# Releasing the projection matmuls before the state decay, and keeping the mixer output in halves

## The chip, the cores and the metric

The kernel runs on the 8 NeuronCores of one Trainium2 chip. All cores run the same program on different data and don't talk to each other. The metric is device time in microseconds of the slowest core, from one execution of the whole program. In all texts PE is TensorE, DVE is VectorE, ACT is ScalarE, POOL is GpSimd and SP is SyncE.

## The reference, cut to what matters

For x of shape (4, 4096, 1024), with 4 heads of width 256:

```
xn = layernorm(x)
q, k, v = silu(xn Wq^T), silu(xn Wk^T), silu(xn Wv^T)      # per head 256 wide
f = log_sigmoid(xn Wf^T) / 8 ;  s = 1 - exp(f)
S1[t] = S1[t-1] * exp(f[t]) + k[t] (x) s[t] ;  ok = q . S1
qv = softmax(ok)
S2[t] = S2[t-1] * exp(f[t]) + s[t] (x) v[t] ;  ov = qv . S2
attn = rmsnorm(silu(ov)) * g_w @ Wo^T
out = x + attn + ffn(xn)      # ffn with quantized weights and activations, inner width 4096
```

## The kernel before

A core takes one batch entry (two cores share one) and runs three stages. Stage 1 (to about 1023 us) quantizes the three FFN weight matrices. Stage 2, the mixer, goes over all 4096 tokens twice: pass `hpg` 0 handles heads 0 and 1, pass 1 handles heads 2 and 3. A pass is a loop over 32 chunks of 128 tokens. Stage 3 (from about 3733 us) is the FFN, the output projection and the sum for the core's own 2048 tokens.

Each engine executes its own instructions in the order in which the program emits them, and engines wait for each other by counting semaphores. Nothing reorders the work: what stands first in the code of an engine holds up all that follows on it. In iteration `c` of a pass the code is emitted in this order:

- `emit_LN(c+1)`: POOL issues the load of the x block (L394), DVE takes the statistics (L403 to L411), ACT takes a square root (L418), DVE writes the normalized block (L430), SP issues its transposing DMA (L441). An x block has two buffers, so the load for chunk c+1 can be issued once chunk c-1 has been normalized.
- `chainA(c-1, 0)`, which starts the part of the previous chunk that doesn't depend on earlier chunks.
- `emit_A2a(c)`: on PE the projections F and K of this chunk, 16 matmuls of 512 columns into `ps_f` and `ps_k` (L467). They wait for the transposed x block and for the mark `M[c-1]["state"]`. Then ACT computes softplus from F (L476, L478), PE forms its cumulative sum and its column sum (L486 into `ps_g`, L488 into `ps_m2`), ACT takes four exponentials (L496 to L502), PE projects Q and V (L511 into `ps_q`, 32 matmuls of 128 columns, and L516 into `ps_v`, 8 of 512), PE turns the total decay into a column and spreads it over the partitions (L528, L532, again into `ps_g`), ACT takes the SiLU of Q, K and V (L540 to L542), DVE forms the gated `stb` (L553 to L557), PE transposes K (L568).
- `chainB` to `chainE` of chunk c-1 for both heads: score, softmax over the 256 slots (ACT L717), second read-out, SiLU into `ov_sb` (ACT L804). Between them `emit_B1_mm(c)` computes the state update of this chunk into `ps_q`, `ps_k`, `ps_v` and `ps_f`, the same four PSUM banks that the projections use.
- `emit_B1_vec(c)` on DVE: for each of the two heads 4 additions of the update in PSUM to the running state (L611, L616, into the buffer `tmpu`) and then 8 multiplications by the decay, which write the f32 state and its bf16 copy (L625 to L638). The multiplications of `s1` read the decay from `ps_g`. The end of all is `M[c]["state"]`.

So the projections of chunk c+1 have to wait for DVE, since the additions read the banks that they overwrite. A helper `S.guard` makes an engine wait for its own last instruction; each head has one between its additions and its multiplications, and one stands between the heads.

`ov_sb` holds the output of a whole pass, 4 blocks of 128 x 4096 in bf16 (4 MB). It is cleared at the start of a pass (L375), together with the states, and written to DRAM by one DMA at its end (L883). The four projection weights of pass 2 are loaded behind that DMA on the same queue, and so is the first x block; the first x block of stage 3 is issued once the last such DMA has landed.

Of the kernel before, what the change touches and what calls it, by code (L numbers as in the profile page):

```python
# [7 lines left out]
F32 = mybir.dt.float32  # L8
F32R = mybir.dt.float32r
BF16 = mybir.dt.bfloat16  # L10
# [5 lines left out]
T = 4096  # L16
# [32 lines left out]
def build_nc(nch=NCH, do_ffn=True, do_ag=True, dbg=(), mix_stop=0):  # L49
# [20 lines left out]
    d_ccout = nc.dram_tensor("cc_out", [1024, T], BF16)  # L70
# [9 lines left out]
    with es:  # L80
# [18 lines left out]
        block = es.enter_context(nc.Block())  # L99
# [227 lines left out]
        s2f = sbB("s2f", [128, 1024], F32)  # L327
        s1b = sbB("s1b", [128, 3 * 1024], BF16)
        s2b = sbB("s2b", [128, 3 * 1024], BF16)
        tmpu = sbB("tmpu", [128, 1024], F32)  # L330
        sf = tmpu[:, 512:1024]
        ov_sb = sbB("ov_sb", [128, 4 * T], BF16)

        ps_q = pstB("ps_q", [128, 512])
        ps_k = pstB("ps_k", [128, 512])
# [13 lines left out]
        dump_marks = []  # L349
        mk_state = 0  # L350
        for hpg in range(1 if mix_stop else 2):
# [28 lines left out]
            M = {}  # L380
# [68 lines left out]
            def emit_A2a(c):  # L449
# [4 lines left out]

                @block.tensor
                def _(t, pp=pp, c=c, gi=gi,
                      mk_prev=M.get(c - 1, {}).get("state", mk_state0h)):
                    S.wait(t, f"qt{pp}", mk_xnT_hist[gi])
                    S.wait(t, "dv", mk_prev)
                    if c == 0:  # L460
                        S.wait(t, "qw", mk_wload_h)
                        S.wait(t, "gp", mk_masks)
                        if dump_marks:
                            S.wait(t, "qst", dump_marks[-1])
                    for dst_ps, wsb in ((ps_f, wf_b), (ps_k, wk_b)):
                        for dc in range(8):
                            i = t.matmul(out=dst_ps[:], lhsT=xnTs(dc),  # L467
                                         rhs=wsb[:, dc * 512:(dc + 1) * 512],
                                         start=(dc == 0), stop=(dc == 7))
                        S.inc(i, "pe")  # L470
# [9 lines left out]
                mk_spf = S.val("sc")  # L480

                @block.tensor
                def _(t, mk_spf=mk_spf, mk_pst=M.get(c - 1, {}).get("st", 0)):
                    S.wait(t, "sc", mk_spf)
                    S.wait(t, "dv", mk_pst)
                    t.matmul(out=ps_g[:], lhsT=utones[:], rhs=spf[:],  # L486
                             start=True, stop=True)
                    i = t.matmul(out=ps_m2[0:1, 0:512], lhsT=ones_col[:], rhs=spf[:],  # L488
                                 start=True, stop=True)
                    S.inc(i, "pe")  # L490
# [110 lines left out]
            def emit_B1_vec(c):  # L601
                wsl = (c % 3) * 1024
                mk_u = M[c]["u"]

                @block.vector
                def _(v, mk_u=mk_u, wsl=wsl):
                    for h, (pu1, pu2) in enumerate(((ps_q, ps_k), (ps_v, ps_f))):
                        S.wait(v, "pe", mk_u - 1 + h)
                        for dkh in range(2):
                            sl = slice(h * 512 + dkh * 256, h * 512 + (dkh + 1) * 256)  # L610
                            v.tensor_tensor(out=tmpu[:, dkh * 256:(dkh + 1) * 256],  # L611
                                            in0=pu1[:, dkh * 256:(dkh + 1) * 256],
                                            in1=s1f[:, sl], op=ALU.add)
                        for mh in range(2):
                            sl = slice(h * 512 + mh * 256, h * 512 + (mh + 1) * 256)
                            i = v.tensor_tensor(out=tmpu[:, 512 + mh * 256:768 + mh * 256],  # L616
                                                in0=pu2[:, mh * 256:(mh + 1) * 256],
                                                in1=s2f[:, sl], op=ALU.add)
                        S.guard(v, i, "dv")
                        for dkh in range(2):  # L620
                            sl = slice(h * 512 + dkh * 256, h * 512 + (dkh + 1) * 256)
                            slw = slice(wsl + h * 512 + dkh * 256,
                                        wsl + h * 512 + (dkh + 1) * 256)
                            ts = tmpu[:, dkh * 256:(dkh + 1) * 256]
                            v.tensor_tensor(out=s1f[:, sl], in0=ts,  # L625
                                            in1=ps_g[:, h * 256:(h + 1) * 256],
                                            op=ALU.mult)
                            v.tensor_tensor(out=s1b[:, slw], in0=ts,  # L628
                                            in1=ps_g[:, h * 256:(h + 1) * 256],
                                            op=ALU.mult)  # L630
                        for mh in range(2):
                            sl = slice(h * 512 + mh * 256, h * 512 + (mh + 1) * 256)
                            slw = slice(wsl + h * 512 + mh * 256,
                                        wsl + h * 512 + (mh + 1) * 256)
                            ts = tmpu[:, 512 + mh * 256:768 + mh * 256]
                            v.tensor_scalar_mul(out=s2f[:, sl], in0=ts,
                                                scalar1=dccol[:, h * 2 + mh:h * 2 + mh + 1])
                            i = v.tensor_scalar_mul(out=s2b[:, slw], in0=ts,  # L638
                                                    scalar1=dccol[:, h * 2 + mh:h * 2 + mh + 1])
                        if h == 0:  # L640
                            S.guard(v, i, "dv")
                        else:
                            S.inc(i, "dv")
                M[c]["state"] = S.val("dv")

            def chainA(c, h, mk_extra=0):
# [125 lines left out]
            def chainE(c, h):  # L772
                sl2 = (c % 2) * 512
                hs = sl2 + h * 256
                rsl = ((c - 1) % 3) * 1024

                @block.tensor
                def _(t, h=h, hs=hs, mk_btm=M[c][f"btm{h}"], rsl=rsl):
                    S.wait(t, "dv", mk_btm)
                    for vh in range(2):  # L780
                        t.matmul(out=ps_i[:, 256 + vh * 128:256 + (vh + 1) * 128],
                                 lhsT=Vb[:, hs + vh * 128:hs + (vh + 1) * 128],
                                 rhs=btm[:], start=True, stop=False)
                        for mh in range(2):
                            i = t.matmul(out=ps_i[:, 256 + vh * 128:256 + (vh + 1) * 128],
                                         lhsT=s2b[:, rsl + h * 512 + mh * 256 + vh * 128:
                                                  rsl + h * 512 + mh * 256 + (vh + 1) * 128],
                                         rhs=qtT[:, mh * 128:(mh + 1) * 128],
                                         start=False, stop=(mh == 1))
                    S.inc(i, "pe")  # L790
                mk_ovp = S.val("pe")

                @block.vector
                def _(v, mk_ovp=mk_ovp):
                    S.wait(v, "pe", mk_ovp)
                    i = v.tensor_copy(out=eok[:], in_=ps_i[:, 256:512])  # L796
                    S.inc(i, "dv")
                mk_ove = S.val("dv")

                @block.scalar  # L800
                def _(sc, h=h, c=c, mk_ove=mk_ove):
                    S.wait(sc, "dv", mk_ove)
                    for vh in range(2):
                        i = sc.activation(  # L804
                            out=ov_sb[:, (2 * h + vh) * T + c * 128:
                                      (2 * h + vh) * T + (c + 1) * 128],
                            in_=eok[:, vh * 128:(vh + 1) * 128],
                            func=AF.Silu)
                    S.inc(i, "sc")

            emit_LN(0)
            for c in range(nch):
# [38 lines left out]
                if c >= 1:  # L851
# [4 lines left out]
                    chainD(c - 1, 1, stc)  # L856
                    chainE(c - 1, 1)
                emit_B1_vec(c)
            if mix_stop:
                mk_state = mk_state0h  # L860
            else:
# [16 lines left out]
            @block.gpsimd  # L878
            def _(g, hpg=hpg):
                S.wait(g, "dv", S.val("dv"))  # L880
                S.wait(g, "sc", S.val("sc"))
                S.wait(g, "qst", S.val("qst"))
                g.dma_start(out=d_ccout.ap()[hpg * 512:(hpg + 1) * 512, :]  # L883
                            .rearrange("(g p) t -> p g t", p=128),
                            in_=ov_sb[:].rearrange("p (g t) -> p g t", g=4)
                            ).then_inc(S.h["qst"], 16)
            S.c["qst"] += 16
            dump_marks.append(S.val("qst"))


# [637 lines left out]
```

## Time and profile before

| | us |
|---|---|
| median of 2 runs | 6448.29 (6443.7 to 6452.88) |
| the profiled execution | 6462.67 |
| its span on the slowest core, core 4 | 6461.1 |
| spans of the 8 cores | 6414.4 to 6461.1 |

Rows of a timeline give the start in us from the span's start and the duration in us; several equal instructions in sequence are merged (x8), and the bracket says how long the engine had been idle before and what it waited for. Rows of a group give busy us and mean ns of one, and after the bar the idle time just before them. The ends of matmuls are modelled and can overlap by some tenths of a us. The granted clock is given as a share of 2.4 GHz, so 0.50 is 1.2 GHz.

### The profile page before, as it was taken

Reading aid. Unit: us, or ns where it says so; the run is one execution under the profiler, and the core shown is the slowest. Engines: PE = TensorE matmul, PEld = TensorE weight load, DVE = VectorE, ACT = ScalarE, POOL = GpSimd, SP = SyncE. Lnnn points to the kernel's source line nnn. Section 1 sums busy time; section 2 is a strip of 40 time slices with the busy share of each in tenths; the row PEclk is TensorE's granted clock in tenths of the full one; section 3 lists DMA queues with packets and bytes.
Section 4 is the critical chain, followed back from the end, with each engine's and each line's share of the span. In section 5 each row is a group of like instructions: output and inputs, shape, how many; then the busy total and the mean of one; then the engine's idle time right before and its main releaser. Section 6 shows DMA issues by size and latency. Waiting matters only on the chain.

```text
span 6461.1 us, 37843 instructions; the slowest of 8 cores (6414.4 to 6461.1 us)
## 1 busy us (share of the span) xinstructions
PE 2429.7 (38%) x10934; PEld 1081.2 (17%) x10934; DVE 2156.4 (33%) x4980; ACT 1436.4 (22%) x2000; POOL 335.4 (5%) x583
## 2 busy tenths in 40 slices
PE   0000002444444424444444425552545254624553
PEld 0000001222222212222222212110211121111111
DVE  2222213444444444444444432213231323132222
ACT  0000001444444424444444412001210021001200
POOL 0000110000000000000000000110001000100010
PEclk9999999666666656666666667656765587557755
DMA  4443223000000021000000021222113211312131
GB/s 149 162 155 128 92 88 78 20 20 20 20 20 20 17 57 28 20 20 20 20 20 20 9 88 52 59 78 65 52 52 91 59 54 48 96 53 62 49 86 51
DMA packets 201145, 371.57 MB, mean 58 GB/s; under 512 B 127216, under 2 KB 135408, under 8 KB 193776
## 3 DMA queue, kind: packets, MB, share of 16 engines
q0 software_dynamic: 80880, 331.39, 16.1%
q1 hardware_dynamic: 120064, 37.76, 2.8%
q8 instruction: 94, 1.54, 0.1%
q14 instruction: 107, 0.88, 0.0%
HBM read 314.58 MB, written 41.94 MB: 55 GB/s over the span
## 4 chain that ended last, share of the span: by engine, by line
PE 26%; DMA 26%; DVE 25%; ACT 13%; issue 9%; DVEq 1%; POOLq 0%; ACTq 0%; SPq 0%; POOL 0%
DMA wdslab<-wdq_s 6%; PE pd L1109 5%; PE pd L1299 4%; DMA wtmp<-wdT 4%; PE pd L1115 3%; PE ps_f L467 3%; DMA wslab<-wuq_s 3%; DMA wslab<-wgq_s 3%; ACT L717 3%; DMA wtmp<-wuT 2%; DMA wtmp<-wgT 2%; DVE mpart L207 2%; DVE tmpu L611 1%; ACT L1127 1%; DVE s1b L628 1%
## 5 line engine op out<-in xcount | busy, mean ns | idle before, releaser
L1109 PE MATMUL pd<-xqTg,wslab 128*128 128x512 bf16 x1024 | 362.8, 518 | 768.3 <-DVE guT L1145 290.2
L1299 PE MATMUL pd<-wdslab,gcvt 128*128 128x512 bf16 x1024 | 452.0, 596 | 357.9 <-DMA wdslab<-wdq_s 236.6
L467 PE MATMUL ps_f<-wf_b,xnT 128*128 128x512 bf16 x512 | 227.0, 624 | 916.0 <-DVE s2b L638 514.6
L418 ACT ACT_TABLE_LOAD x64 | 82.1, 1283 | 1633.5 <-DVE lncol L411 1633.5
L1145 DVE TENSOR_TENSOR guT<-pd,sgT 128x512 f32<-128x512 f32 x128 | 88.5, 692 | 847.9 <-ACT sgT L1127 847.9
L1127 ACT ACT_TABLE_LOAD x128 | 164.2, 1283 | 898.2 <-PE pd L1115 898.2
L804 ACT ACT_TABLE_LOAD x128 | 164.2, 1283 | 622.2 <-DVE eok L796 622.2
L1416 ACT ACT_TABLE_LOAD x16 | 20.5, 1283 | 1255.9 <-DVE rrow L1407 1255.9
L1115 PE MATMUL pd<-xqTg,wslab 128*128 128x512 bf16 x1024 | 284.0, 427 | 0.0
L1109 PEld LDWEIGHTS pd<-xqTg,wslab 128*128 128x128 bf16 x1024 | 114.6, 120 | 990.3 <-issue 952.6
L223 PE MATMUL ps_w<-ones_col,mcol 128*1 128x1 f32 x6 | 0.6, 163 | 733.9 <-DVE mcol L216 733.9
L1287 DVE CAST gcvt<-guqT 128x256 bf16<-128x256 int8 x256 | 74.5, 293 | 589.7 <-PE pd L1299 589.3
L739 PE MATMUL ps_m<-identb,qtb 128*128 128x128 bf16 x256 | 47.6, 288 | 532.4 <-DVE qtb L727 532.4
L467 PEld LDWEIGHTS ps_f<-wf_b,xnT 128*128 128x128 bf16 x512 | 66.5, 139 | 1036.8 <-issue 1036.8
L1299 PEld LDWEIGHTS pd<-wdslab,gcvt 128*128 128x128 bf16 x1024 | 110.8, 125 | 697.6 <-issue 691.8
L280 DVE TENSOR_SCALAR wi<-wtmp,swcol 128x1024 int8<-128x1024 f32 (+1 forms) x48 | 61.7, 1286 | 457.0 <-DMA wtmp<-wdT 233.7
L717 ACT ACT_TABLE_LOAD x128 | 164.2, 1283 | 221.0 <-DVE smcol L699 221.0
L207 DVE TENSOR_REDUCE mpart<-wtmp 128x1 f32<-128x1024 f32 (+1 forms) x48 | 109.8, 2286 | 290.5 <-DMA wtmp<-wdT 140.3
L1276 POOL DMA_DIRECT2D wdslab<-wdq_s x256 | 138.0, 539 | 865.6 <-PE pd L1299 865.6
L553 DVE COPY dccol<-ps_m 128x4 f32<-128x4 f32 x64 | 10.4, 162 | 486.9 <-PE ps_g L532 486.9
L467 PE MATMUL ps_k<-wk_b,xnT 128*128 128x512 bf16 x512 | 156.4, 460 | 0.0
L394 POOL DMA_DIRECT2D xin<-x x64 | 34.0, 532 | 2251.2 <-DVE stT L670 2213.8
(194 smaller groups left out, 5017.3 us busy)
## 6 DMA issues: line engine op xcount, KB each, us to landing
wdslab<-wdq_s POOLq DMA_DIRECT2D x256, 256.0 KB, 2.9
wtmp<-wgT POOLq DMA_DIRECT2D x16, 2048.0 KB, 8.9
wtmp<-wuT POOLq DMA_DIRECT2D x16, 2048.0 KB, 8.8
wtmp<-wdT POOLq DMA_DIRECT2D x64, 512.0 KB, 3.5
xin<-x POOLq DMA_DIRECT2D x64, 512.0 KB, 5.0
wslab<-wgq_s POOLq DMA_DIRECT2D x32, 1024.0 KB, 6.1
wslab<-wuq_s POOLq DMA_DIRECT2D x32, 1024.0 KB, 6.1
wgq_s<-wqb POOLq DMA_DIRECT2D x8, 1024.0 KB, 4.1
```

The costliest lines, as they stand in the source:

```text
L207: i = v.reduce_sum(out=mpart[:, it:it + 1], in_=wtmp[:, :tw], axis=AXX, apply_absolute_value=True)
L418: i = sc.activation(out=lncol[:, 3:4], in_=lncol[:, 6:7], func=AF.Sqrt)
L467: i = t.matmul(out=dst_ps[:], lhsT=xnTs(dc), rhs=wsb[:, dc * 512:(dc + 1) * 512], start=(dc == 0), stop=(dc == 7))
L717: i = sc.activation(out=eok[:], in_=okf[:], func=AF.Exp, bias=smcol[:, 0:1], accum_out=smcol[:, 1:2])
L804: i = sc.activation(out=ov_sb[:, (2 * h + vh) * T + c * 128: (2 * h + vh) * T + (c + 1) * 128], in_=eok[:, vh * 128:(vh + 1) * 128], func= ...
L1109: i = t.matmul(out=pd[0][:, 0:512], lhsT=wslab[:, gbase + dc * 512 + isl * 128: gbase + dc * 512 + (isl + 1) * 128], rhs=xqTg[:, dc * GTOK ...
L1115: i = t.matmul(out=pd[0][:, 512:1024], lhsT=wslab[:, ubase + dc * 512 + isl * 128: ubase + dc * 512 + (isl + 1) * 128], rhs=xqTg[:, dc * G ...
L1127: i = sc.activation(out=sgT[:], in_=pd[0][:, 0:512], func=AF.Silu, scale=inv_swg[:])
L1145: i = v.tensor_tensor(out=guT[:, sl_id * GTOK:(sl_id + 1) * GTOK], in0=pd[0][:, 512:1024], in1=sgT[:], op=ALU.mult)
L1276: g.dma_start(out=wdslab[:, ppd * 1024:(ppd + 1) * 1024], in_=d_wdq[dc * 128:(dc + 1) * 128, :]).then_inc(S.h[f"qd{ppd}"], 16)
L1287: i = v.tensor_copy(out=gcvt[:, ppd * 256:(ppd + 1) * 256], in_=guqT[:, dc * GTOK + sg * 256: dc * GTOK + (sg + 1) * 256])
L1299: i = t.matmul(out=pd[sg * 2 + bi2][:, half * 512:(half + 1) * 512], lhsT=gcvt[:, ppd * 256 + bi2 * 128: ppd * 256 + (bi2 + 1) * 128], rhs ...
```

## The change

In `emit_B1_vec` the DVE work is split. All 8 additions of both heads come first, into a buffer `tmpa` of twice the size (each head has its own half), and their end is a new mark `M[c]["uev"]`. DVE then waits once for its own additions and does all 16 multiplications; their end remains `M[c]["state"]`. The number and the shapes of the DVE operations are the same; of the three own waits one is left.

The F and K projections of the next chunk now wait for `uev` instead of `state`. The cumulative-sum matmul, which overwrites `ps_g`, now waits for `state` (before, for the earlier mark `st`, since the projections ahead of it had waited for `state`).

`ov_sb` now holds half a pass (2 MB). In iteration 16, after `emit_B1_vec(16)`, POOL waits for ACT's last SiLU and writes the first half to DRAM; ACT waits for that DMA before it writes the output of chunk 16. The second half is written at the end of the pass. In POOL's program the new DMA stands ahead of the load of the x block of chunk 18.

```diff
@@ -327,9 +327,9 @@
         s2f = sbB("s2f", [128, 1024], F32)
         s1b = sbB("s1b", [128, 3 * 1024], BF16)
         s2b = sbB("s2b", [128, 3 * 1024], BF16)
-        tmpu = sbB("tmpu", [128, 1024], F32)
-        sf = tmpu[:, 512:1024]
-        ov_sb = sbB("ov_sb", [128, 4 * T], BF16)
+        tmpa = sbB("tmpa", [128, 2048], F32)
+        sf = tmpa[:, 1536:2048]
+        ov_sb = sbB("ov_sb", [128, 2 * T], BF16)
 
         ps_q = pstB("ps_q", [128, 512])
         ps_k = pstB("ps_k", [128, 512])
@@ -454,7 +454,7 @@
 
                 @block.tensor
                 def _(t, pp=pp, c=c, gi=gi,
-                      mk_prev=M.get(c - 1, {}).get("state", mk_state0h)):
+                      mk_prev=M.get(c - 1, {}).get("uev", mk_state0h)):
                     S.wait(t, f"qt{pp}", mk_xnT_hist[gi])
                     S.wait(t, "dv", mk_prev)
                     if c == 0:
@@ -480,7 +480,7 @@
                 mk_spf = S.val("sc")
 
                 @block.tensor
-                def _(t, mk_spf=mk_spf, mk_pst=M.get(c - 1, {}).get("st", 0)):
+                def _(t, mk_spf=mk_spf, mk_pst=M.get(c - 1, {}).get("state", 0)):
                     S.wait(t, "sc", mk_spf)
                     S.wait(t, "dv", mk_pst)
                     t.matmul(out=ps_g[:], lhsT=utones[:], rhs=spf[:],
@@ -603,25 +603,34 @@
                 mk_u = M[c]["u"]
 
                 @block.vector
-                def _(v, mk_u=mk_u, wsl=wsl):
+                def _(v, mk_u=mk_u):
                     for h, (pu1, pu2) in enumerate(((ps_q, ps_k), (ps_v, ps_f))):
                         S.wait(v, "pe", mk_u - 1 + h)
+                        ub = h * 1024
                         for dkh in range(2):
                             sl = slice(h * 512 + dkh * 256, h * 512 + (dkh + 1) * 256)
-                            v.tensor_tensor(out=tmpu[:, dkh * 256:(dkh + 1) * 256],
+                            v.tensor_tensor(out=tmpa[:, ub + dkh * 256:ub + (dkh + 1) * 256],
                                             in0=pu1[:, dkh * 256:(dkh + 1) * 256],
                                             in1=s1f[:, sl], op=ALU.add)
                         for mh in range(2):
                             sl = slice(h * 512 + mh * 256, h * 512 + (mh + 1) * 256)
-                            i = v.tensor_tensor(out=tmpu[:, 512 + mh * 256:768 + mh * 256],
+                            i = v.tensor_tensor(out=tmpa[:, ub + 512 + mh * 256:
+                                                         ub + 768 + mh * 256],
                                                 in0=pu2[:, mh * 256:(mh + 1) * 256],
                                                 in1=s2f[:, sl], op=ALU.add)
-                        S.guard(v, i, "dv")
+                        S.inc(i, "dv")
+                M[c]["uev"] = S.val("dv")
+
+                @block.vector
+                def _(v, wsl=wsl, mk_uev=M[c]["uev"]):
+                    S.wait(v, "dv", mk_uev)
+                    for h in range(2):
+                        ub = h * 1024
                         for dkh in range(2):
...
@@ -632,15 +641,12 @@
...
                             v.tensor_scalar_mul(out=s2f[:, sl], in0=ts,
                                                 scalar1=dccol[:, h * 2 + mh:h * 2 + mh + 1])
                             i = v.tensor_scalar_mul(out=s2b[:, slw], in0=ts,
                                                     scalar1=dccol[:, h * 2 + mh:h * 2 + mh + 1])
-                        if h == 0:
-                            S.guard(v, i, "dv")
-                        else:
-                            S.inc(i, "dv")
+                    S.inc(i, "dv")
                 M[c]["state"] = S.val("dv")
 
             def chainA(c, h, mk_extra=0):
@@ -800,10 +806,15 @@
                 @block.scalar
                 def _(sc, h=h, c=c, mk_ove=mk_ove):
                     S.wait(sc, "dv", mk_ove)
+                    HCH = T // 2 // 128
+                    if c == HCH and dump_marks:
+                        S.wait(sc, "qst", dump_marks[-1])
+                    ch = c % HCH
+                    TH = T // 2
                     for vh in range(2):
                         i = sc.activation(
-                            out=ov_sb[:, (2 * h + vh) * T + c * 128:
-                                      (2 * h + vh) * T + (c + 1) * 128],
+                            out=ov_sb[:, (2 * h + vh) * TH + ch * 128:
+                                      (2 * h + vh) * TH + (ch + 1) * 128],
                             in_=eok[:, vh * 128:(vh + 1) * 128],
                             func=AF.Silu)
                     S.inc(i, "sc")
@@ -856,6 +867,17 @@
                     chainD(c - 1, 1, stc)
                     chainE(c - 1, 1)
                 emit_B1_vec(c)
+                if c - 1 == T // 2 // 128 - 1:
+                    @block.gpsimd
+                    def _(g, hpg=hpg):
+                        S.wait(g, "sc", S.val("sc"))
+                        S.wait(g, "qst", S.val("qst"))
+                        g.dma_start(out=d_ccout.ap()[hpg * 512:(hpg + 1) * 512, 0:T // 2]
+                                    .rearrange("(g p) t -> p g t", p=128),
+                                    in_=ov_sb[:].rearrange("p (g t) -> p g t", g=4)
+                                    ).then_inc(S.h["qst"], 16)
+                    S.c["qst"] += 16
+                    dump_marks.append(S.val("qst"))
             if mix_stop:
                 mk_state = mk_state0h
             else:
@@ -880,11 +902,19 @@
                 S.wait(g, "dv", S.val("dv"))
                 S.wait(g, "sc", S.val("sc"))
                 S.wait(g, "qst", S.val("qst"))
-                g.dma_start(out=d_ccout.ap()[hpg * 512:(hpg + 1) * 512, :]
+                hoff = T // 2 if nch > T // 2 // 128 else 0
+                g.dma_start(out=d_ccout.ap()[hpg * 512:(hpg + 1) * 512,
+                                             hoff:hoff + T // 2]
                             .rearrange("(g p) t -> p g t", p=128),
                             in_=ov_sb[:].rearrange("p (g t) -> p g t", g=4)
                             ).then_inc(S.h["qst"], 16)
-            S.c["qst"] += 16
+                if nch <= T // 2 // 128:
+                    g.dma_start(out=d_ccout.ap()[hpg * 512:(hpg + 1) * 512,
+                                                 T // 2:T]
+                                .rearrange("(g p) t -> p g t", p=128),
+                                in_=ov_sb[:].rearrange("p (g t) -> p g t", g=4)
+                                ).then_inc(S.h["qst"], 16)
+            S.c["qst"] += 16 if nch > T // 2 // 128 else 32
             dump_marks.append(S.val("qst"))
 
 
```

## Rows read from the trace of the kernel before

**Rows 1.** The page: its head.

```profile
span 6461.1 us, 37843 instructions; the slowest of 8 cores (6414.4 to 6461.1 us)
```

**Rows 2.** Chain that ended last, 1700 to 1790 us: shares by line.

```profile
by line: PE ps_f L467 11.8%; issue 7.9%; ACT L717 5.7%; DVE tmpu L611 4.2%; DVE s1b L628 3.9%; DVE s1f L625 3.8%; DVE tmpu L616 3.7%; DVE s2b L638 3.3%; PE ps_k L467 3.2%; DVE s2f L636 2.9%; ACT L496 2.9%; ACT L476 2.9%; ACT eok L717 2.7%; 
```

**Rows 3.** Timeline of DVE, one chunk: start us, us, operation [idle before <-releaser].

```profile
1736.27 0.74 DVE L611 TENSOR_TENSOR tmpu<-ps_q,s1f 128x256 f32<-128x256 f32 x2
...
1737.78 0.42 DVE L625 TENSOR_TENSOR s1f<-tmpu,ps_g 128x256 f32<-128x256 f32 x1
...
1740.41 0.76 DVE L611 TENSOR_TENSOR tmpu<-ps_v,s1f 128x256 f32<-128x256 f32 x2 [0.17 <-DVE s2b L638]
...
1741.93 0.42 DVE L625 TENSOR_TENSOR s1f<-tmpu,ps_g 128x256 f32<-128x256 f32 x1
...
1744.32 0.68 DVE L403 BATCH_NORM_STATS2 lnst<-xin 128x6 f32<-128x512 f32 x1
```

**Rows 4.** Timeline of ACT, the same chunk.

```profile
1747.80 0.20 ACT L418 ACTIVATE lncol<-lncol 128x1 f32<-128x1 f32 x1
1748.11 1.28 ACT L476 ACT_TABLE_LOAD   x1
```

**Rows 5.** ACT, exp table load for F: its group (busy, mean ns | idle), one timeline row.

```profile
L476 ACT ACT_TABLE_LOAD x64 | 82.1, 1283 | 40.5 <-PE ps_f L467 40.0
...
2313.83 1.28 ACT L476 ACT_TABLE_LOAD   x1 [9.97 <-PE ps_f L467]
```

**Rows 6.** Timeline of PE, the same chunk.

```profile
1744.55 3.48 PE L467 MATMUL ps_f<-wf_b,xnT 128*128 128x512 bf16 x8 [8.30 <-DVE s2b L638]
1747.86 1.89 PE L467 MATMUL ps_k<-wk_b,xnT 128*128 128x512 bf16 x8
1750.97 0.47 PE L486 MATMUL ps_g<-spf,utones 128*128 128x512 f32 x1 [1.22 <-ACT spf L478]
...
1753.31 1.89 PE L516 MATMUL ps_v<-wv_b,xnT 128*128 128x512 bf16 x8
1755.45 1.02 PE L528 MATMUL ps_m<-one_one,dcrow 1*128 1x1 f32 x8 [0.25 <-ACT etmp L502]
...
1758.45 0.58 PE L568 MATMUL ps_m<-identb,Kb 128*128 128x128 bf16 x4 [1.64 <-DVE stb L557]
```

**Rows 7.** Granted clock of stretches: from:to us, length, PE busy (x), PEclk, DMA share, GB/s.

```profile
1751.50:1755.20 3.70, 3.70 (x41) 1.00 0.71 196
1763.80:1764.20 0.40, 0.33 (x2) 0.50 0.00 0
```

**Rows 8.** Page, part 5: first TensorE work after the softmax of each head.

```profile
L739 PE MATMUL ps_m<-identb,qtb 128*128 128x128 bf16 x256 | 47.6, 288 | 532.4 <-DVE qtb L727 532.4
```

**Rows 9.** Groups by line on PE, both passes: xcount | busy us, mean ns | idle before.

```profile
L467 PE MATMUL ps_f<-wf_b,xnT 128*128 128x512 bf16 x512 | 227.0, 624 | 916.0 <-DVE s2b L638 514.6 <-DMA xnT<-xnbf 334.1 <-DVE xnbf L430 67.2
L467 PE MATMUL ps_k<-wk_b,xnT 128*128 128x512 bf16 x512 | 156.4, 460 | 0.0
```

**Rows 10.** Timeline of PE: a long F/K burst.

```profile
1096.69 3.57 PE L467 MATMUL ps_f<-wf_b,xnT 128*128 128x512 bf16 x8 [7.67 <-DVE s2b L638]
1100.06 3.19 PE L467 MATMUL ps_k<-wk_b,xnT 128*128 128x512 bf16 x8
```

**Rows 11.** Timeline, turn from pass 1 to pass 2.

```profile
2370.80 0.76 POOL L883 DMA_DIRECT2D cc_out<-ov_sb  x1 [175.48 <-ACT ov_sb L804]
...
2385.60 0.91 DVE L372 MEMSET s1f<- 128x1024 f32 x1 [17.31 <-DMA cc_out<-ov_sb]
...
2392.75 0.88 POOL L359 DMA_DIRECT2D wk_b<-wkT  x1 [20.29 <-issue]
...
2424.57 0.69 DVE L403 BATCH_NORM_STATS2 lnst<-xin 128x6 f32<-128x512 f32 x1 [13.49 <-DMA xin<-x]
```

**Rows 12.** Page, part 6: DMA issues, KB each, median us to landing.

```profile
wtmp<-wgT POOLq DMA_DIRECT2D x16, 2048.0 KB, 8.9
...
xin<-x POOLq DMA_DIRECT2D x64, 512.0 KB, 5.0
```

More of the change, by code:

```diff
@@ L623, in _ @@
                                         wsl + h * 512 + (dkh + 1) * 256)
-                            ts = tmpu[:, dkh * 256:(dkh + 1) * 256]
+                            ts = tmpa[:, ub + dkh * 256:ub + (dkh + 1) * 256]
                             v.tensor_tensor(out=s1f[:, sl], in0=ts,
@@ L634, in _ @@
                                         wsl + h * 512 + (mh + 1) * 256)
-                            ts = tmpu[:, 512 + mh * 256:768 + mh * 256]
+                            ts = tmpa[:, ub + 512 + mh * 256:ub + 768 + mh * 256]
                             v.tensor_scalar_mul(out=s2f[:, sl], in0=ts,
```

## The prediction

> **What bounds the kernel now.** I read three views. The page's head [rows 1] gives the span, 6461.1 us; the execution took 6462.7, the median of the runs is 6448.3. The chain of waits inside the mixer [rows 2] is the one to look at, since the change lies there. No line has more than 12%; PE, ACT and DVE follow each other in small pieces, so a chunk is one long dependency loop and its length is the sum of the pieces. In this loop stands all of the DVE state update, L611 to L638. Then the timelines of one chunk. DVE works on the update from 1736.27 to 1744.32, which is 8.05 us, and goes straight on to the layer norm of the chunk after [rows 3]. PE sits idle for 8.30 us until the update's last instruction and starts F/K at 1744.55 [rows 6]. So 8.28 us lie between the start of the update and F/K.
>
> The reader is to see a second thing there. ACT's program has the square root of that layer norm ahead of the exponential of F. In this chunk the root starts at 1747.80, takes 0.20, and the table load for the exponential starts at 1748.11 with no idle time marked [rows 4]. Over both passes ACT waited 40.0 us for F at this place, in 64 times [rows 5]. Four of these are the first and the last chunk of each pass, 9.97 us in the last one [rows 5], where no layer norm stands ahead. The rest comes to some 0.15 us per chunk. F and the root arrive together. F is moved ahead by this change, the root isn't.
>
> **Part 1: DVE.** The work is the same, less two of three own waits. An own wait between the heads shows as 0.17 us idle [rows 3]. Four additions with a wait behind them take 1.51 (1736.27 to 1737.78), without it about 1.33; eight multiplications take 2.39 (1741.93 to 1744.32) [rows 3]. New order: 1.33 + 1.52 = 2.85 to the end of the additions, then 2 x 2.39 = 4.78, in all 7.63. The layer norm starts 0.42 earlier. F/K starts 0.2 behind the additions, at about 3.0 instead of 8.28, so 5.3 earlier.
>
> **Part 2: what F/K's 5.3 us are worth.** The cumulative-sum matmul L486 started at 1750.97, 6.65 after the layer norm [rows 3, 6]. All of this is root, table load and two ACT functions in a row. It now starts at 7.63 + 6.65 = 14.28 after the update's start instead of 14.70. With the 0.15 that ACT still waited for F, the gain is 0.57 us per chunk; the other 4.7 us turn into idle time of PE. L486's new wait for `state` costs nothing: that mark comes at 7.6. If the root were not in the way, it would be 5.3. In the last chunk of each pass, where ACT had waited 9.97 for F, nothing is in the way, and the gain is 5.3: two chunks, -10.6 us.
>
> **Part 3: the idle time and TensorE's clock.** Before, PE waited 1.22 us between K and L486 [rows 6], and Q and V ran at granted clock 1.00, which is 2.4 GHz [rows 7]. F/K now ends at 3.0 + 5.2 to 6.6 and L486 comes at 14.3, so the gap grows to 4.7 to 6.1 us. The nearest rows are the waits for the softmax: 532.4 us before 128 such places, 4.16 each [rows 8], and the work behind one has clock 0.50, which is 1.2 GHz [rows 7]. F/K itself, after 8.30 us, starts slow too (8 matmuls in 3.48, where K's 8 take 1.89 [rows 6]). The new gap lies between the two, so I expect L486, Q and V to begin at 1.2 GHz. The Trainium skill (TensorE: Matmul & The Clock Gate, Part 1: The HAM clock gate) has the rule that the clock halves after idle time and is earned back only by sustained work, which speaks against starting F/K early; the trace agrees in the clock of 0.50 just named.
>
> The price: V ended at 1755.20, L528 started at 1755.45, 4.48 after L486, and was released by ACT, 0.25 after V [rows 6]. So Q and V are hidden by a hair. L486, L488, Q and V stream as many columns as F/K plus two of its matmuls. F/K, from a slow start, took 5.20 here [rows 6], 6.56 in a long case [rows 10] and 5.99 in the mean (227.0 + 156.4 over 64 [rows 9]). Two more matmuls at the fast rate (K's 8 in 1.89 [rows 6]) add 0.4: 5.6, 7.0 and 6.4 from L486 to the end of V. I take 5.6, a choice: before, a late rise of the clock did not lengthen the chunk, now it does, and this moves the next burst to another place; I expect that to settle at the short end, but no row shows it. L528 then starts 5.6 after L486, +1.12. What follows, 3.00 us to L568 [rows 6], is taken as unchanged.
>
> Per chunk: -0.57 + 1.12 = +0.55. There are 62 chunks with a predecessor, two of them counted above, so 60 x 0.55 = +33. Bounds: no fall of the clock, -0.57; the mean restart, +1.35; all long, +1.95.
>
> **Part 4: the halves.** The 4 MB write took from 2370.80 to 2385.60, 14.8 us, and what is behind it on the queue waits: the load of wq landed before 2392.75, 7.2 after [rows 11]. 2 MB take 8.9 [rows 12], so each of the two pass ends gains 5.9: -12. Clearing half of `ov_sb` is worth nothing, as DVE then waits 13.49 for the x block anyway [rows 11]. In the middle, POOL issues the first half 2 to 3 us after the update of chunk 16 begins (ACT's last SiLU) and only then the x block of chunk 18, which was issued a chunk earlier before. With 8.9 for the write and part of 5.0 for the block [rows 12] it lands at 12 to 17, and DVE wants it at 7.6. I take 4.5 late, twice: +9. Bounds 0 and 9 each.
>
> **Sum.** +33 - 10.6 - 12 + 9 = +19. The profiled execution would go from 6462.7 to 6482, the median from 6448.3 to 6468.
>
> **The rivals.** (a) The full gain: the root is not what L486 waits for. 62 x -5.3 - 3 = -332, 6117. Against it stands the order of ACT's program and its 0.15 us of waiting. Chance 0.04. (b) The clock does not fall in the gap, and Q and V stay hidden: 60 x -0.57 - 13.6 = -48, 6400. Against it: gaps of 4.16 and of 8.30 us both ended in slow work. Chance 0.06. (c) Slower by over 2%: the clock does not rise within Q and V at all. A slow matmul of 512 columns takes 0.42 (8 in 3.37 [rows 10]), 18 take 7.6, so +3.1 - 0.57 = +2.5 per chunk, +139, 6587. It decides from 7.4 us between L486 and L528, where 60 x 2.38 - 13.6 reaches 129 us. Against it: the clock rose inside F/K in the cases shown [rows 6, 9]. Chance 0.04. (d) The burst restarts at the mean or longer: +1.35 x 60 - 13.6 = +67, 6516; the long end 6552. It belongs to my forecast's mechanism; chance 0.29. The forecast itself, 6440 to 6500, has 0.57.
>
> **How the numbers follow.** The range reaches from (b) to most of (d): 6405 to 6530. Only (a) is faster by over 2% (129 us, about what a measurement of this kernel can tell from no change), only (c) and a mishap in the middle are slower: 0.05, 0.91, 0.04.
>
> **What would show it.** Right: F/K starts about 3 us after the update's first addition; the wait before the exponential's table load for F is gone; L486's idle is about 5 us, released by ACT's `spf`; Q and V show clock 0.50 at their start; L528 follows V without idle; one stall of DVE for `xin` in each pass. Wrong: if L486 moves by 5 us in every chunk, part 2 is wrong; if V still ends 4.2 us after L486, part 3 is; if the x block of chunk 18 is there in time or tens of us late, part 4 is.

## The result, and the profile after

| | us | runs |
|---|---|---|
| before | 6447.5 median (6443.7 to 6452.9) | 6 |
| changed | 6520.6 median (6514.5 to 6531.1) | 7 |

The ratio is 1.0113, with a 95% interval of 1.0101 to 1.0126. The change makes the kernel slower by 1.1%, 73 us, which is within 2%. The forecast was 6468, in a range of 6405 to 6530.

Where the 73 us lie can be read from the traces of both kernels, as means over the 8 cores. Stage 1 takes 1075.7 and 1077.0 us up to the first F/K, pass 1 takes 1360.4 and 1393.7, pass 2 to the first statistics of the FFN 1315.7 and 1351.6, the rest 2681 and 2687. So 69 us are in the mixer.

The timeline of DVE in one chunk after the change (start us, us, operation, bracket: idle before). The additions now stand ahead:

```profile
2859.48 0.74 DVE L612 TENSOR_TENSOR tmpa<-ps_q,s1f 128x256 f32<-128x256 f32 x2
...
2861.47 0.74 DVE L617 TENSOR_TENSOR tmpa<-ps_f,s2f 128x256 f32<-128x256 f32 x2
2862.31 0.42 DVE L634 TENSOR_TENSOR s1f<-tmpa,ps_g 128x256 f32<-128x256 f32 x1
...
2867.07 0.68 DVE L403 BATCH_NORM_STATS2 lnst<-xin 128x6 f32<-128x512 f32 x1
```

The update takes 7.59 us instead of 8.05 [rows 3]. The layer norm, L403, starts only 0.46 earlier. PE in the same chunk:

```profile
2862.36 3.57 PE L467 MATMUL ps_f<-wf_b,xnT 128*128 128x512 bf16 x8 [2.90 <-DVE tmpa L617]
2865.72 2.90 PE L467 MATMUL ps_k<-wk_b,xnT 128*128 128x512 bf16 x8
2873.64 0.77 PE L486 MATMUL ps_g<-spf,utones 128*128 128x512 f32 x1 [5.01 <-ACT spf L478]
2874.20 0.63 PE L488 MATMUL ps_m<-spf,ones_col 128*1 128x512 f32 x1
2874.64 3.57 PE L511 MATMUL ps_q<-xnT,wq_b 128*128 128x128 bf16 x32
2878.04 1.89 PE L516 MATMUL ps_v<-wv_b,xnT 128*128 128x512 bf16 x8
2879.86 1.05 PE L528 MATMUL ps_m<-one_one,dcrow 1*128 1x1 f32 x8
2880.78 0.47 PE L532 MATMUL ps_g<-dcrow,ones_row 1*128 1x512 f32 x1
2883.14 0.38 PE L568 MATMUL ps_m<-identb,Kb 128*128 128x128 bf16 x4 [1.89 <-ACT Vb L542]
```

F/K starts 2.88 us after the update's first addition, where it had been 8.28 [rows 3, 6]. L486 comes 11.28 after F/K instead of 6.42. The idle time ahead of it grew from 1.22 to 5.01 (means of all chunks but the first and the last of a pass: 0.72 and 5.70). L528 follows V without a wait, 6.22 after L486 instead of 4.48, and L568 is now released by ACT's SiLU, 3.28 after L528 instead of 3.00 [rows 6]. ACT in the same chunk:

```profile
2869.26 1.28 ACT L418 ACT_TABLE_LOAD   x1 [7.82 <-DVE lncol L411]
2870.55 0.20 ACT L418 ACTIVATE lncol<-lncol 128x1 f32<-128x1 f32 x1
2870.78 1.28 ACT L476 ACT_TABLE_LOAD   x1
...
2880.01 1.28 ACT L540 ACT_TABLE_LOAD   x1 [1.55 <-PE ps_v L516]
```

F was done in about 3.4 us, by 2866, and ACT was idle. But the instruction next in its program is the root of the layer norm, which waits for DVE until 2869. The exponential's table load comes right behind it, as in [rows 4]. That is where the 5 us went. The granted clock of stretches of the same chunk (from:to us, length, PE busy (x), PEclk, DMA share, GB/s):

```profile
2873.60:2875.00 1.40, 1.36 (x6) 0.50 1.24 217
2875.00:2877.00 2.00, 2.00 (x22) 0.50 0.60 218
2877.00:2879.80 2.80, 2.80 (x20) 0.82 0.00 1
```

After the longer idle time L486 and most of Q run at 0.50, which is 1.2 GHz; the clock rises to 1.00 at the end of Q, and 0.82 is the mean of a stretch that holds both. Before, Q and V ran at 1.00 [rows 7]. The groups of the whole mixer (busy us, mean ns, bar, idle before; the first row is of the kernel before, the others are after the change) say that it isn't this chunk alone:

```profile
L511 PE MATMUL ps_q<-xnT,wq_b 128*128 128x128 bf16 x2048 | 125.5, 219 | 0.0
...
L511 PE MATMUL ps_q<-xnT,wq_b 128*128 128x128 bf16 x2048 | 209.2, 294 | 0.0
L476 ACT ACT_TABLE_LOAD x64 | 82.1, 1283 | 21.0 <-PE ps_f L467 19.9
L540 ACT ACT_TABLE_LOAD x64 | 82.1, 1283 | 91.6 <-PE ps_v L516 91.5
L486 PE MATMUL ps_g<-spf,utones 128*128 128x512 f32 x64 | 47.8, 746 | 345.9 <-ACT spf L478 345.9
```

ACT's idle time ahead of the table load for F fell from 40.0 [rows 5] to 19.9, all of it in the first and the last chunk of each pass. New are 91.5 us in which ACT waits for V.

### The profile page after: what moved, and what is told of

The parts are those of the page before. It is cut to its first block, busy times and chain, and to the rows that moved or that the text cites. A ratio compares the mean times of both kernels' runs of the same rounds, so it can differ in the third digit from the quotient of the medians.

```text
span 6529.5 us, 37725 instructions; the slowest of 8 cores (6495.2 to 6529.5 us)
## 1 busy us (share of the span) xinstructions
PE 2528.9 (39%) x10934; PEld 1167.8 (18%) x10934; DVE 2130.5 (33%) x4980; ACT 1436.3 (22%) x2000; POOL 336.7 (5%) x585
## 4 chain that ended last, share of the span: by engine, by line
PE 26%; DMA 26%; DVE 24%; ACT 12%; issue 10%; DVEq 1%; POOLq 0%; ACTq 0%; SPq 0%; POOL 0%
DMA wdslab<-wdq_s 5%; PE pd L1139 4%; PE pd L1329 4%; DMA wtmp<-wdT 4%; PE pd L1145 3%; DMA wslab<-wgq_s 3%; PE ps_q L511 3%; DMA wslab<-wuq_s 3%; ACT L723 3%; DMA wtmp<-wuT 2%; DMA wtmp<-wgT 2%; PE ps_v L516 2%; DVE mpart L207 2%; ACT L1157 1%; PE pd L1479 1%
## 5 line engine op out<-in xcount | busy, mean ns | idle before, releaser
L1139 PE MATMUL pd<-xqTg,wslab 128*128 128x512 bf16 x1024 | 351.5, 505 | 776.9 <-DVE guT L1175 289.0
L1145 PE MATMUL pd<-xqTg,wslab 128*128 128x512 bf16 x1024 | 279.1, 422 | 0.0
L511 PE MATMUL ps_q<-xnT,wq_b 128*128 128x128 bf16 x2048 | 209.2, 294 | 0.0
L511 PEld LDWEIGHTS ps_q<-xnT,wq_b 128*128 128x128 bf16 x2048 | 196.2, 141 | 45.2 <-issue 45.2
```

Source lines behind the costliest of these rows:

```text
L511: i = t.matmul(out=ps_q[:, j * 128:(j + 1) * 128], lhsT=wq_b[:, dc * 512 + j * 128:dc * 512 + (j + 1) * 128], rhs=xnTs(dc), start=(dc == 0 ...
L1139: i = t.matmul(out=pd[0][:, 0:512], lhsT=wslab[:, gbase + dc * 512 + isl * 128: gbase + dc * 512 + (isl + 1) * 128], rhs=xqTg[:, dc * GTOK ...
L1145: i = t.matmul(out=pd[0][:, 512:1024], lhsT=wslab[:, ubase + dc * 512 + isl * 128: ubase + dc * 512 + (isl + 1) * 128], rhs=xqTg[:, dc * G ...
```

## The experiments

All times below stand beside runs of the kernel before on the same chip; their median was 6453.3 us for the first four and 6450.1 for the others, 6 and 3 us above the 6447.5 of the result. Experiments 1, 4 and 5 ended 1 to 2 us above the ranges expected for them. "Mixer" is the sum of both passes as above, the mean over 8 cores: 2676 us before, 2745 changed.

**1. Only the halves.** The kernel before with `ov_sb` of 2 MB and the additional write, nothing else. The split update was not run by itself with the whole `ov_sb`, so its share is the difference between this kernel and the changed one.

```diff
-        ov_sb = sbB("ov_sb", [128, 4 * T], BF16)
+        ov_sb = sbB("ov_sb", [128, 2 * T], BF16)
...
```

> The kernel before with only the mixer output kept in halves; the state update and all waits are as before. My theory: two pass ends gain 5.9 us each, two stalls of DVE for the x block of chunk 18 cost about 5 us each (4.9 and 5.4 were read in the changed kernel), so about -2 us against before: 6440 to 6450. Rival: the halves carry the loss of 73 us, then about 6520.

Measured: 6450.8, ratio 0.9994 (0.9984 to 1.0005), mixer 2675. The halves are neutral, so the 73 us come with the split; that is an inference from the difference. In the one chunk of each pass where the x block is late (DVE timeline of this kernel),

```profile
1755.88 0.69 DVE L403 BATCH_NORM_STATS2 lnst<-xin 128x6 f32<-128x512 f32 x1 [3.68 <-DMA xin<-x]
```

the chunk is 5.2 us longer than its neighbours, more than the 3.68 of the stall. PE shows why:

```profile
1762.47 0.48 PE L486 MATMUL ps_g<-spf,utones 128*128 128x512 f32 x1 [4.74 <-ACT spf L478]
1762.77 0.60 PE L488 MATMUL ps_m<-spf,ones_col 128*1 128x512 f32 x1
1763.18 3.40 PE L511 MATMUL ps_q<-xnT,wq_b 128*128 128x128 bf16 x32
```

With the idle time ahead of L486 at 4.74, Q takes 3.40 instead of 1.96. It is the loss of the change in a kernel that doesn't have the split. L486 itself still took 0.48, as before: here the clock fell only after PE had resumed.

**2. Dead work in the gap.** The changed kernel with 20 matmuls after K in chunks 1 to 30 of each pass, whose result nobody reads.

```diff
+                if 1 <= c < nch - 1:
...
+                        for _k in range(20):
+                            t.matmul(out=ps_m2[:], lhsT=xnTs(0),
+                                     rhs=wk_b[:, 0:512], start=True, stop=True)
```

> The changed kernel with 20 dead matmuls of 512 columns after K in chunks 1 to 30, into a bank that nobody reads at that time. They fill about 4.3 of the 5.5 us in which PE waits for softplus. Clock theory: Q and V run at full clock again, from L486 to L528 4.5 us instead of 6.2 and to the transpose of K 3.0 instead of 3.28, so -2.0 us in 58 chunks against the changed kernel: about 6400. Rival: Q and V are slow for another reason (PSUM, reads of the weights, DVE running beside them): no change, about 6520, or more.

Measured: 6434.7, ratio 0.9973 (0.9962 to 0.9985), so 86 us less than the changed kernel, and the mixer at 2633 is 112 us shorter. PE's wait ahead of the cumulative sum, and Q (groups of this kernel, both passes):

```profile
L492 PE MATMUL ps_g<-spf,utones 128*128 128x512 f32 x64 | 30.7, 480 | 95.1 <-ACT spf L484 95.0
...
L517 PE MATMUL ps_q<-xnT,wq_b 128*128 128x128 bf16 x2048 | 129.8, 223 | 0.0
```

Q is back at 129.8 us from 209.2 (125.5 before). From the cumulative sum to L528 it is 4.58 in the mean, near the 4.48 before, and 3.0 from there to L568. More work on PE made the kernel faster, and the mean granted clock of the cores rose from 0.716 to 0.743, so it was the clock. Where the wait was longer, it wasn't so: in one chunk (at 3466 us) it was 2.39, and Q took 2.94. The expectation of 6400 was missed in the total, not in the mixer (2.0 us in 58 chunks, 116, expected; 112 measured): stage 1, which has the same instructions, took 1100 us instead of 1077 in the mean of the eight cores. DVE's waits for its weight loads there grew from 750 to 773 us. Why is open.

**3. The root out of the way.** The changed kernel; `emit_LN` is cut in three. ACT's root is emitted behind the SiLUs of `emit_A2a(c)`, DVE's last two instructions and the transposing DMA inside `chainB`, where DVE waits for the softmax.

```diff
                 emit_A2a(c)
+                if c + 1 < nch:
+                    emit_LNroot(c + 1)
                 if c >= 1:
-                    chainB(c - 1, 0)
+                    chainB(c - 1, 0, (lambda: emit_LNend(c + 1)) if c + 1 < nch else None)
...
```

> The changed kernel with ACT's square root of the layer norm moved behind the SiLU of Q, K and V, and DVE's end of the layer norm moved into its wait for the softmax. Root theory: the exponential of F follows F at once, L486 comes 6.5 us after F/K instead of 11.3, the gap ahead of it is some 1.2 us again, Q and V run at full clock: -5.3 us per chunk against before, about 6120. Rival: the root was not what L486 waited for (DVE's multiplications or PSUM hold it): 6500 or more.

Measured: 6110.4, ratio 0.9473 (0.9455 to 0.949), mixer 2332. PE in one chunk of this kernel:

```profile
1697.27 3.57 PE L477 MATMUL ps_f<-wf_b,xnT 128*128 128x512 bf16 x8 [2.90 <-DVE tmpa L627]
1700.63 2.27 PE L477 MATMUL ps_k<-wk_b,xnT 128*128 128x512 bf16 x8
1703.78 0.47 PE L496 MATMUL ps_g<-spf,utones 128*128 128x512 f32 x1 [0.88 <-DVE lncol L406]
...
1704.33 1.96 PE L521 MATMUL ps_q<-xnT,wq_b 128*128 128x128 bf16 x32
1706.13 1.89 PE L526 MATMUL ps_v<-wv_b,xnT 128*128 128x512 bf16 x8
1708.27 1.02 PE L538 MATMUL ps_m<-one_one,dcrow 1*128 1x1 f32 x8 [0.25 <-ACT etmp L512]
```

and ACT:

```profile
1700.92 1.28 ACT L486 ACT_TABLE_LOAD   x1 [4.51 <-PE ps_f L477]
...
1710.41 0.60 ACT L552 ACTIVATE Vb<-ps_v 128x512 bf16<-128x512 f32 x1
1711.03 1.28 ACT L421 ACT_TABLE_LOAD   x1
1712.33 0.20 ACT L421 ACTIVATE lncol<-lncol 128x1 f32<-128x1 f32 x1
1713.72 1.28 ACT L733 ACT_TABLE_LOAD   x1 [1.19 <-DVE lncol L437]
```

The exponential waits for F alone, the cumulative sum comes 6.51 after F/K, the gap is 0.88, Q takes 1.96, and from the cumulative sum to L538 it is 4.49 as in [rows 6]. (The profile puts the gap down to DVE's L406. The kernel waits there for ACT's `spf` and for `state`, the end of the multiplications, which DVE had passed at 1702; ACT's L488 ends at 1703.53, so it was ACT.) The root costs nothing at its new place: ACT still waits 1.19 us ahead of the softmax. A chunk takes 35.05 us in the mean; it took 40.47 before and 41.8 after the change.

**4. The root moved in the kernel before.** The same edit on the kernel before.

> The kernel before with the same move of the root. Root theory: there F, not the root, comes last by 0.15 us, so nothing is gained: 6435 to 6450. Rival: the root's place alone is worth several us per chunk: below 6300.

Measured: 6452.3, ratio 1.0002 (0.9992 to 1.0012). The move alone is worth nothing, the split with the halves costs 73 us, both together gain 343. Each of the two conditions of the exponential hid the other.

**5. Q and V in the gap.** The changed kernel with the PE block of Q and V (L511, L516) emitted ahead of L486. It is the same text, moved.

```diff
+                @block.tensor
+                def _(t, pp=pp, xnTs=xnTs):
+                    ...
                 @block.tensor
                 def _(t, mk_spf=mk_spf, mk_pst=M.get(c - 1, {}).get("state", 0)):
```

> The changed kernel with the matmuls of Q and V moved ahead of L486 in PE's program, so that real work fills PE's wait for softplus. Clock theory: F, K, Q and V together take about 9.3 us of the 11.3 up to L486, V no longer stands behind it, L528 comes 4.5 us after L486 and the transpose of K 3.0 after that, as in the kernel before: about -1.9 us per chunk against the changed kernel, and two last chunks lose 3 us each, so 6410 to 6430. Rival: L528 comes later for another reason than V's place and clock: above 6480.

Measured: 6432.3, ratio 0.9972 (0.9961 to 0.9983), mixer 2658, 88 less than the 2745 of the changed kernel. L528 comes 4.5 after L486 and L568 3.0 after that, as expected. The gain, 1.6 us per chunk in the mean, is smaller than the 1.9 expected. Some of it is given back: the small matmuls behind L528 now run at the low clock (L528, timeline of this kernel):

```profile
1763.61 1.83 PE L528 MATMUL ps_m<-one_one,dcrow 1*128 1x1 f32 x8 [3.78 <-ACT etmp L519]
```

1.83 us instead of 1.02, and from L568 to the next update 18.5 instead of 18.2 in the mean. The mean granted clock of this kernel's cores, 0.712, is not higher than that of the changed one, 0.716, though it is 88 us faster. What counts is the clock of the work on the path.

**6. A smaller dose.** As 2, with `range(8)`.

> As with 20 dead matmuls, but 8: the idle time ahead of L486 is then about 3.8 us instead of 1.2. A dose between: where PE's gap is short enough the clock stays at 2.4 GHz, else it falls. If a gap of 3.8 us is as bad as the 4.16 us ahead of the softmax transposes, nothing is gained and the mixer stays at 6.2 us from L486 to L528 (about 6520); if it is harmless, 4.5 us (about 6420). I expect it to lie in between, nearer to the bad end: 5.5 to 6.0 us.

Measured: 6498.6, ratio 1.0079 (1.0064 to 1.0095), mixer 2724, 5.99 us from the cumulative sum to L528 in the mean, within the 5.5 to 6.0 expected. The groups of this kernel:

```profile
L517 PE MATMUL ps_q<-xnT,wq_b 128*128 128x128 bf16 x2048 | 211.8, 296 | 0.0
...
L492 PE MATMUL ps_g<-spf,utones 128*128 128x512 f32 x64 | 37.9, 592 | 235.0 <-ACT spf L484 235.0
```

The gap is 235.0/64, some 3.7 us in the mean, and Q is as slow as with 5.4 (345.9/64). With 95.1/64, 1.5 us, it is fast in nearly all chunks. What did get faster is the cumulative sum: 592 ns in the mean where it was 746. One of its chunks shows why, first PE, then the granted clock:

```profile
2075.61 0.47 PE L492 MATMUL ps_g<-spf,utones 128*128 128x512 f32 x1 [3.29 <-ACT spf L484]
...
2076.16 3.25 PE L517 MATMUL ps_q<-xnT,wq_b 128*128 128x128 bf16 x32
```

```profile
2075.60:2076.10 0.50, 0.49 (x2) 1.00 0.96 182
2077.00:2079.60 2.60, 2.60 (x24) 0.50 0.46 172
```

After 3.29 us of idle time the clock is still at 1.00 when PE resumes, and it falls while Q already runs; it is like this in about half of the chunks. So a fast first matmul behind a gap doesn't mean that the work behind it is fast.

**7 and 8. The write of the first half behind the x block.** The block that writes the first half is emitted one step later, behind the load for chunk 18, once in the kernel of experiment 3 and once in the changed kernel.

```diff
                     emit_LN(c + 1)
+                if c - 2 == T // 2 // 128 - 1:
+                    @block.gpsimd
+                    ...
```

> The kernel with the late root, and the first half of the mixer output written behind the load of the x block of chunk 18 instead of ahead of it. The two stalls of about 5 us go, nothing else changes: about -10 us against the kernel with the late root, 6095 to 6105. Rival: the stalls come from the write's share of the DMA engines and stay: 6110.

> The changed kernel with the same move of the write of the first half. Two stalls of 4.9 and 5.4 us of DVE go: about -10 us against the changed kernel, 6505 to 6515. Rival: no change.

Measured on the changed kernel: 6507.5, ratio 1.0091 (1.0079 to 1.0104), 13 us less than the changed kernel, mixer 2734, 11 to 12 less. The two stalls are gone. Measured with the late root: 6102.7, ratio 0.9464 (0.9451 to 0.9477), and the mixer stays at 2331. Here my expectation of 10 us was wrong: the total lies within the 6095 to 6105 that I gave, but the mixer, where the gain was to be, has none, and the two ratios can't be told apart. The stall was there in experiment 3, as DVE's timeline shows:

```profile
1671.34 0.69 DVE L403 BATCH_NORM_STATS2 lnst<-xin 128x6 f32<-128x512 f32 x1 [4.38 <-DMA xin<-x]
...
1674.71 0.16 DVE L563 COPY dccol<-ps_m 128x4 f32<-128x4 f32 x1 [0.68 <-PE ps_g L542]
```

but with the root late nobody waits for these statistics early. DVE still reaches the next instruction that needs PE, L563, 0.68 us ahead of it, so the 4.38 us of stall are hidden. The kernels of experiments 3 and 7 are the fastest, 5.3 and 5.4% below the kernel before.

## Why the prediction was right, and where it was off

**Part 1, DVE.** Right. 7.59 us against 7.63, F/K at 2.88 against 3.0.

**Part 2, the root.** Right, and this was the decisive step. L486 comes 2.88 + 11.28 = 14.16 after the update's start, against 14.28. Experiment 3 shows that it is the root: with it, and with DVE's end of the layer norm, which waits for it, out of the way, L486 follows F/K by 6.5. The two last chunks, with no layer norm ahead, gained as forecast: L486 follows F/K by 6.52 in both. Rival (a), the full gain, is excluded for this kernel and is what experiment 3 has. Experiment 4 confirms that F had been just behind the root, as the 0.15 us of waiting [rows 5] had said.

**Part 3, the clock.** The mechanism was right: the clock falls in the gap (rival (b) is out), and it rises within Q and V (rival (c) is out). The size was off. The step that failed is the choice of 5.6 us between L486 and L528. It was 6.2 in the mean, from 5.5 to 7.1. The argument that the burst would settle at the short end was wrong. A long case (PE, changed kernel):

```profile
2830.99 0.76 PE L486 MATMUL ps_g<-spf,utones 128*128 128x512 f32 x1 [5.87 <-ACT spf L478]
...
2835.41 2.70 PE L516 MATMUL ps_v<-wv_b,xnT 128*128 128x512 bf16 x8
2838.05 1.05 PE L528 MATMUL ps_m<-one_one,dcrow 1*128 1x1 f32 x8
```

That is 7.06, and the chunk after it has 6.22. The lengths go through cycles of three to five chunks. The mean of the F/K rows plus two matmuls, 6.4, would have been the better value; it was one of the three in the text (rival (d), which said 6516). The measured 6520.6 is outside the 6440 to 6500 that I thought most likely; it is rival (d) that came true, with the 0.29 that I gave it. (K's rate gives 0.47 for two matmuls and not 0.4, so the sum itself should have been 5.7; that is 4 us in all.) The second miss in this part is "what follows is taken as unchanged": with V late, ACT's SiLU releases L568, and 3.00 became 3.28.

By chunk: -0.6 for L486 (14.20 after the update's start in experiment 8, which has no stalls, against 14.81 before, in the mean), +1.72 for L528, +0.28 for L568, in all +1.4; measured 41.84 (without the two stalled chunks' extra) against 40.47. Times 60 it is 82 us. The forecast had 33.

**Part 4, the halves.** Right in sum (-5 us against the -3 forecast), by errors that cancel in part. At the turn of the passes DVE went on 10.7 us after the write of 2 MB was issued, not 8.9, but the weight loads behind it were also somewhat shorter, so that the turn, from the write to the first statistics, took 44.5 instead of 53.8 (POOL and DVE, changed kernel):

```profile
2413.95 0.76 POOL L906 DMA_DIRECT2D cc_out<-ov_sb  x1 [174.54 <-ACT ov_sb L815]
...
2458.49 0.69 DVE L403 BATCH_NORM_STATS2 lnst<-xin 128x6 f32<-128x512 f32 x1 [16.93 <-DMA xin<-x]
```

That is 9.2 us instead of the 5.9 forecast [rows 11]; why the weight loads are shorter is not tested. The stalls were as placed, behind the write, at 4.84 and about 5.4 us (forecast 4.5); the first:

```profile
1763.39 0.76 POOL L875 DMA_DIRECT2D cc_out<-ov_sb  x1 [114.30 <-ACT ov_sb L815]
1764.14 1.05 POOL L394 DMA_DIRECT2D xin<-x  x2
...
1773.32 0.69 DVE L403 BATCH_NORM_STATS2 lnst<-xin 128x6 f32<-128x512 f32 x1 [4.84 <-DMA xin<-x]
```

**Sum.** 82 for the chunks, some 10 less for the two last chunks, 10 more for the stalls, 15 less at the two pass ends: 67, against 69 measured in the mixer. Of the 53 us between forecast and result, 49 are the size of part 3.

## What to carry to other kernels

When a wait is released earlier, look at what stands next in the program of the engine that consumes the result. Here an unrelated square root, queued ahead, turned 5 us of head start into 5 us of idle time, and moving it made the same change worth 5%. An idle time that is made longer isn't free on TensorE: price the work behind it at both clocks, and ask whether that work was hidden by much or by a hair. Two conditions that end within 0.2 us of each other must be moved together; moving either alone gained nothing here.

## What the runs showed of the hardware

- TensorE's clock after idle time: with waits of 1.5 us in the mean ahead of the burst (experiment 2) Q ran at 2.4 GHz in nearly all chunks; with 3.7 (experiment 6) and 5.4 us (changed kernel) in the mean, and with the one of 4.7 shown in experiment 1, it ran at 1.2 GHz for the most part. In the changed kernel the restart made 5.5 to 7.1 us out of the 4.48 from L486 to L528.
- The fall need not come within the wait: in experiment 6 the clock was still 1.00 after 3.29 us of idle time and fell to 0.50 within 1.4 us of PE's resuming.
- The Trainium skill (TensorE: Matmul & The Clock Gate, Part 1: The HAM clock gate) has it that the clock is at half after idle time and that sustained work brings it back. The rows agree in both: 0.50 from 2873.60 to 2877.00, behind 5.01 us of idle time, and 1.00 again by the end of Q.
- A DMA issued behind another of 2 MB on POOL's queue landed behind it: the x block, which takes 5.0 us in the median [rows 12], was there for DVE 9.2 us after its issue (1764.14 to 1773.32).
- Stage 1 of the kernel with 20 dead matmuls per chunk took 23 us more in the mean of the cores, though its instructions there are the same. No run explains it.
